# An eight-core transformer layer: one shared SBUF arena split by data type, rotary tables kept in DRAM, three attention panel buffers in place of four

## The reference

```python
x = L0_attn_x                                   # (4, 4096, 2048) float32
x = x + layernorm(attn(layernorm(x)))           # latent attention, 16 heads of 128, causal
x = x + layernorm(ffn(layernorm(x)))            # int8 weights with scales, 8192 wide

def attn(x):
    q = x @ Wq + bq
    kv = x @ Wdown                              # 2048 -> 512
    k, v = kv @ Wk_up, kv @ Wv_up               # 512 -> 2048
    q, k = q*cos + rotate_half(q)*sin, k*cos + rotate_half(k)*sin
    p = softmax(causal(q @ k.T / sqrt(128)))
    return (p @ v) @ Wo + bo

def ffn(x):
    return (silu((x @ w_gate)*s_gate) * ((x @ w_up)*s_up)) @ w_down * s_down
```

## Time and profile before

| | us |
|---|---|
| median of 2 runs | 6633.36 |
| lowest and highest | 6477.97, 6788.75 |
| the profiled execution, whole time | 6477.97 |
| its span on the slowest core (core 3) | 6476.4 |
| spans of the 8 cores | 6450.2 to 6476.4 |
| PE busy in the span | 4436.6 (69%) |
| DVE, ACT, POOL busy | 1560.7, 1398.4, 824.7 |

### The profile page before, as it was taken

How to read it: one execution, slowest core, us unless ns; L and a number is a source line. 1 busy time by engine, 2 the same in 40 slices (tenths; PEclk the granted TensorE clock), 3 DMA queues, 4 the chain that set the end, 5 groups by cost and what they waited for, 6 DMA issues and landing times.

```text
span 6476.4 us, 67826 instructions; the slowest of 8 cores (6450.2 to 6476.4 us)
## 1 busy us (share of the span) xinstructions
PE 4436.6 (69%) x21376; PEld 2020.8 (31%) x21376; DVE 1560.7 (24%) x2965; ACT 1398.4 (22%) x3067; POOL 824.7 (13%) x956
## 2 busy tenths in 40 slices
PE   0144344386666666645546998699986999879985
PEld 0011111132333333422212443244432444334432
DVE  0243334254333333323331110111102110021101
ACT  0212211012666666632221010011001100011000
POOL 0021112142000000000001111111111111111111
PEclk9877677697777777767778999899998999989998
DMA  8423332623777777762229995599947996499944
GB/s 185 114 89 103 96 102 87 142 58 92 146 148 148 151 147 147 151 154 86 83 94 159 151 155 133 137 165 153 149 127 156 156 149 131 127 166 156 150 124 130
DMA packets 1541560, 858.04 MB, mean 132 GB/s; under 512 B 776930, under 2 KB 1516258, under 8 KB 1525474
## 3 DMA queue, kind: packets, MB, share of 16 engines
q0 software_dynamic: 679296, 434.14, 39.7%
q1 hardware_dynamic: 839842, 327.28, 22.5%
q10 hardware_dynamic: 22080, 92.28, 4.2%
HBM read 373.37 MB, written 109.05 MB: 74 GB/s over the span
## 4 chain that ended last, share of the span: by engine, by line
PE 44%; DMA 19%; DVE 11%; ACT 11%; issue 9%; POOL 3%; SPq 2%; ACTq 0%; DVEq 0%; POOLq 0%
PE ps L1043 14%; PE ps L1057 14%; PE ps L1110 8%; DMA arena<-wd 7%; ACT arena L775 7%; DMA ctxr<-xin 3%; PE ps L873 2%; PE ps L446 2%; DMA arena<-arena 2%; PE ps L747 2%; DVE smalls L769 2%; POOL arena L630 2%; PE ps L708 1%; DVE arena L481 1%; DMA arena<-wo 1%
## 5 line engine op out<-in xcount | busy, mean ns | idle before, releaser
L1043 PE MATMUL ps<-arena 128*128 128x512 bf16 x4096 | 934.5, 382 | 198.3 <-DMA arena<-wg 138.0
L1110 PE MATMUL ps<-arena 128*128 128x512 bf16 x4096 | 916.3, 379 | 141.4 <-DMA arena<-wd 140.7
L1057 PE MATMUL ps<-arena 128*128 128x512 bf16 x4096 | 925.8, 379 | 0.0
L775 ACT ACTIVATE arena<-ps,smalls 128x512 bf16<-128x512 f32 (+1 forms) x1152 | 748.4, 667 | 471.3 <-DVE smalls L769 339.0
L747 PE MATMUL ps<-arena 128*128 128x512 bf16 (+1 forms) x1152 | 485.9, 483 | 416.6 <-ACT arena L775 337.1
L1043 PEld LDWEIGHTS ps<-arena 128*128 128x128 bf16 x4096 | 402.6, 98 | 689.1 <-issue 211.8
L1110 PEld LDWEIGHTS ps<-arena 128*128 128x128 bf16 x4096 | 386.3, 97 | 670.8 <-issue 239.4
L412 PE MATMUL ps<-arena 128*128 128x512 bf16 x512 | 129.5, 417 | 663.2 <-DVE arena L421 427.9
L1073 DVE TENSOR_SCALAR ctxr<-ps,smalls 128x512 bf16<-128x512 f32 x256 | 192.1, 750 | 1500.4 <-PE ps L1057 1500.4
L1057 PEld LDWEIGHTS ps<-arena 128*128 128x128 bf16 x4096 | 400.8, 98 | 483.3
L1068 ACT ACTIVATE ctxr<-ps,smalls 128x512 bf16<-128x512 f32 x256 | 175.9, 687 | 1562.5 <-PE ps L1043 1562.5
(11 more groups left out here) (75 smaller groups left out, 2819.5 us busy)
## 6 DMA issues: line engine op xcount, KB each, us to landing
arena<-wg POOLq DMA_DIRECT2D x128, 1024.0 KB, 7.1
arena<-wu POOLq DMA_DIRECT2D x128, 1024.0 KB, 7.2
arena<-wd POOLq DMA_DIRECT2D x256, 512.0 KB, 3.8
ctxr<-xin SPq DMA_DIRECT2D x32, 1024.0 KB, 5.9
xnf_scr<-arena SPq DMA_DIRECT2D x16, 1024.0 KB, 7.1
k_scr<-ctxr SPq DMA_DIRECT2D x16, 1024.0 KB, 7.1
v_scr<-ctxr SPq DMA_DIRECT2D x16, 1024.0 KB, 7.4
arena<-k_scr ACTq DMA_DIRECT2D x16, 1024.0 KB, 5.8
```

The lines of the kernel that those rows point to most:

```text
L775: s.activation(P_b[par][:, n0:n0 + N], psa[:, 0:N], ACT.Exp, bias=negc[:, par:par + 1], scale=1.0, accum_out=lacc[:, par * 8 + ci: par * 8 ...
L1043: rr = t.matmul(ga, wg_s[slp][:, fc, icw * 128:(icw + 1) * 128], x1nfm[:, fc, :], start=(fc == 0), stop=(fc == NH - 1))
L1057: rr = t.matmul(ua, wu_s[slp][:, fc, icw * 128:(icw + 1) * 128], x1nfm[:, fc, :], start=(fc == 0), stop=(fc == NH - 1))
L1110: rr = t.matmul(psa, f_b[:, quar * 4 + ic, j * 128:(j + 1) * 128], wd_s[qp][:, ic, :], start=(quar == 0 and ic == 0), stop=(quar == 15 and ...
```

## The change

One idea runs through it: on-chip memory is now two tensors of one type each, `arF` (12,800 float32 a partition) and `arB` (45,056 bfloat16), beside `ctxr`; no tile is a bit-cast view any more. The tiles are dealt out anew, and since less fits at a time, four things are done otherwise.

- **Tables.** `build_tbl` reads both parts of the K and the Q tables in pieces of 1024 columns (512 KB each) on SP, DVE adds them, SP writes the sum to new DRAM tensors; one pair of buffers `tb1`, `tb2` serves all 12 pieces (4 + 4 + 2 + 2). All of it stands at the start of stage A, before the `wo` conversion's writes and the loads of x on SP. Stages A and B load the slices of 512 columns that a group or round needs (256 KB each, two a group or round, double-buffered) from the ACT queue. Stage B no longer loads or adds tables. The `wo` conversion goes through `xnfm1`, whose first load need not wait for a table.
- **Attention.** Three `P_b` and three `PT_b` in place of four, `par` counts modulo 3, and the context matmuls are emitted when more than two panels are pending, so behind the scores of the panel two after it.
- **Stage D.** The residual sum is written over `tmpd` (no `x1td`), the second layer norm goes to a bfloat16 tile of its own.
- **Stage E.** `sd_b` is replaced by slices of 256 KB, loaded from the ACT queue at the start of each `og` (16 in all, double-buffered); the last normalization is done in place (no `tmpe`); `f_b` lies in `ctxr`, and the float32 tiles `dout` and `x1te` in `arF`.

The core of the diff:

```diff
+    ck_scr = scratch("ck_scr", [128, SEQ], F32)
+    sk_scr = scratch("sk_scr", [128, SEQ], F32)
+    cq_scr = scratch("cq_scr", [128, TOK], F32)
+    sq_scr2 = scratch("sq_scr2", [128, TOK], F32)
...
-    AR_U = 69632
+    ARF_U = 12800
+    ARB_U = 45056
     CTX_U = 32768
-    arena = e(nc.sbuf_tensor("arena", [128, AR_U], BF16))
+    arF = e(nc.sbuf_tensor("arF", [128, ARF_U], F32))
+    arB = e(nc.sbuf_tensor("arB", [128, ARB_U], BF16))
     ctxr = e(nc.sbuf_tensor("ctxr", [128, CTX_U], BF16))
-    smalls = e(nc.sbuf_tensor("smalls", [128, 512], F32))
+    smalls = e(nc.sbuf_tensor("smalls", [128, 256], F32))
...
-        ca = Carver(arena, AR_U)
-        cosk = ca.take([SEQ], F32)
-        sink = ca.take([SEQ], F32)
-        tblt_off = ca.off
-        tblt = ca.take([SEQ], F32)
-        xnfm_off = ca.off
-        xnfm0 = ca.take([NH, 512], BF16)
-        xnfm1 = ar_view(arena, tblt_off, [NH, 512], BF16)
+        cf = Carver(arF, ARF_U)
+        x_t = [cf.take([DM]) for _ in range(3)]
+        rot = [cf.take([512]) for _ in range(2)]
+        m1 = [cf.take([512]) for _ in range(2)]
+        cslc = [cf.take([512]) for _ in range(2)]
+        sslc = [cf.take([512]) for _ in range(2)]
+        tb1 = cf.take([1024])
+        tb2 = cf.take([1024])
+        ca = Carver(arB, ARB_U)
+        wdn_s = ca.take([NH, LAT])
+        wku_s = ca.take([4, DM])
+        wvu_s = ca.take([4, DM])
+        xnfm0 = ca.take([NH, 512])
+        xnfm1 = ca.take([NH, 512])
         xnfm2 = [xnfm0, xnfm1]
-        kvl2 = [ca.take([4, 512], BF16) for _ in range(2)]
-        rot = [ca.take([512], F32) for _ in range(2)]
-        m1 = [ca.take([512], F32) for _ in range(2)]
-        wdn_s = ca.take([NH, LAT], BF16)
-        wku_s = ca.take([4, DM], BF16)
-        wvu_s = ca.take([4, DM], BF16)
+        kvl2 = [ca.take([4, 512]) for _ in range(2)]
         cc = Carver(ctxr, CTX_U)
-        x_t = [cc.take([DM], F32) for _ in range(3)]
-        xn_tm = [cc.take([DM], BF16) for _ in range(2)]
-        kst = cc.take([NH, 512], BF16)
-        vst = cc.take([NH, 512], BF16)
+        xn_tm = [cc.take([DM]) for _ in range(2)]
+        kst = cc.take([NH, 512])
+        vst = cc.take([NH, 512])
         assert cc.off <= CTX_U
...
-        for dst, hi, lo, slot in ((cosk, ckh, ckl, s_cosk),
-                                  (sink, skh, skl, s_sink)):
-            e1 = st("Q", lambda q, d=dst, h=hi: q.dma_start(d, h), dma="dQ")
-            e2 = st("Q", lambda q, l=lo: q.dma_start(tblt, l),
-                    waits=prod_waits(s_tbl), dma="dQ")
-            ev = st("V", lambda v, d=dst: v.tensor_add(d, d, tblt),
-                    waits=[e1, e2])
-            slot.produced(ev)
-            s_tbl.used(ev)
-
-        tblt_b = ar_view(arena, 16384, [NH, 512], BF16)
+        def build_tbl(hi, lo, dst_scr, width):
+            for s0 in range(0, width, 1024):
+                e1 = st("Q", lambda q, hi=hi, s0=s0: q.dma_start(
+                    tb1, hi[:, s0:s0 + 1024]), waits=prod_waits(s_tb1),
+                    dma="dQ")
+                s_tb1.produced(e1)
+                e2 = st("Q", lambda q, lo=lo, s0=s0: q.dma_start(
+                    tb2, lo[:, s0:s0 + 1024]), waits=prod_waits(s_tb2),
+                    dma="dQ")
+                s_tb2.produced(e2)
+                ev = st("V", lambda v: v.tensor_add(tb1, tb1, tb2),
+                        waits=[e1, e2])
+                s_tb1.produced(ev)
+                s_tb2.used(ev)
+                ew = st("Q", lambda q, d=dst_scr, s0=s0: q.dma_start(
+                    d[:, s0:s0 + 1024], tb1), waits=[ev], dma="dQ")
+                s_tb1.used(ew)
+
+        build_tbl(ckh, ckl, ck_scr, SEQ)
+        build_tbl(skh, skl, sk_scr, SEQ)
+        build_tbl(cqh, cql, cq_scr, TOK)
+        build_tbl(sqh, sql, sq_scr2, TOK)
+
         for og in range(4):
             def fnc(g, og=og):
                 sap = bass.AP(wo.tensor, og * 512,
                               [[DM, 128], [128 * DM, NH], [1, 512]])
-                return g.dma_start(tblt_b, sap)
-            ev = st("G", fnc, waits=prod_waits(s_tbl), dma="dG")
-            s_tbl.produced(ev)
+                return g.dma_start(xnfm1, sap)
+            ev = st("G", fnc, waits=prod_waits(s_xnfm2[1]), dma="dG")
+            s_xnfm2[1].produced(ev)
 
             def fnw(q, og=og):
                 dap = bass.AP(wo_scr.tensor, og * 512,
                               [[DM, 128], [128 * DM, NH], [1, 512]])
-                return q.dma_start(dap, tblt_b)
-            ev = st("Q", fnw, waits=cons_waits(s_tbl), dma="dQ")
-            s_tbl.used(ev)
-        s_xnfm2[1].users = list(s_tbl.users)
-        s_xnfm2[1].ready = list(s_tbl.ready)
+                return q.dma_start(dap, xnfm1)
+            ev = st("Q", fnw, waits=cons_waits(s_xnfm2[1]), dma="dQ")
+            s_xnfm2[1].used(ev)
...
+            ev = st("S", lambda s, kg=kg, kgp=kgp: s.dma_start(
+                cslc[kgp], ck_scr[:, kg * 512:(kg + 1) * 512]),
+                waits=prod_waits(s_cslc[kgp]), dma="dA")
+            s_cslc[kgp].produced(ev)
+            ev = st("S", lambda s, kg=kg, kgp=kgp: s.dma_start(
+                sslc[kgp], sk_scr[:, kg * 512:(kg + 1) * 512]),
+                waits=prod_waits(s_sslc[kgp]), dma="dA")
+            s_sslc[kgp].produced(ev)
...
-        for dst, hi, lo, slot in ((cosq, cqh, cql, s_cosq),
-                                  (sinq, sqh, sql, s_sinq)):
-            e1 = st("Q", lambda q, d=dst, h=hi: q.dma_start(d, h), dma="dQ")
-            e2 = st("Q", lambda q, l=lo: q.dma_start(tbltB, l),
-                    waits=prod_waits(s_tbl), dma="dQ")
-            ev = st("V", lambda v, d=dst: v.tensor_add(d, d, tbltB),
-                    waits=[e1, e2])
-            slot.produced(ev)
-            s_tbl.used(ev)
-
         def bload(r):
             rp = r % 2
+            ev = st("S", lambda s, r=r, rp=rp: s.dma_start(
+                cslq[rp], cq_scr[:, r * 512:(r + 1) * 512]),
+                waits=prod_waits(s_cslq[rp]), dma="dA")
+            s_cslq[rp].produced(ev)
+            ev = st("S", lambda s, r=r, rp=rp: s.dma_start(
+                sslq[rp], sq_scr2[:, r * 512:(r + 1) * 512]),
+                waits=prod_waits(s_sslq[rp]), dma="dA")
+            s_sslq[rp].produced(ev)
...
-        ccv = Carver(arena, AR_U)
-        k_s = [ccv.take([SEQ], BF16) for _ in range(2)]
-        v_t = [ccv.take([32, 128], BF16) for _ in range(2)]
-        q_s = [ccv.take([TOK], BF16) for _ in range(2)]
-        P_b = [ccv.take([SEQ], BF16) for _ in range(4)]
-        PT_b = [ccv.take([32, 128], BF16) for _ in range(4)]
-        mks_s = ccv.take([NH, 256], F32)
-        ctx = ar_view(ctxr, 0, [NH, DM], BF16)
+        ccv = Carver(arB, ARB_U)
+        k_s = [ccv.take([SEQ]) for _ in range(2)]
+        v_t = [ccv.take([32, 128]) for _ in range(2)]
+        q_s = [ccv.take([TOK]) for _ in range(2)]
+        P_b = [ccv.take([SEQ]) for _ in range(3)]
+        PT_b = [ccv.take([32, 128]) for _ in range(3)]
+        cfv = Carver(arF, ARF_U)
+        mks_s = cfv.take([NH, 256])
+        ctx = ar_view(ctxr, 0, [NH, DM])
 
         s_k = [Slot(), Slot()]
         s_v = [Slot(), Slot()]
         s_q = [Slot(), Slot()]
-        s_P = [Slot() for _ in range(4)]
-        s_PT = [Slot() for _ in range(4)]
+        s_P = [Slot() for _ in range(3)]
+        s_PT = [Slot() for _ in range(3)]
...
-                par = pancnt % 4
+                par = pancnt % 3
...
-                if len(pend) > 3:
+                if len(pend) > 2:
...
-                x1td, tmpd, xtd[xp]),
+                tmpd, tmpd, xtd[xp]),
...
-            eln3 = ln_soup(x1td, tmpd.bitcast(BF16)[:, 0:DM], s_x1, s_tmp,
-                           [ev_w1])
+            eln3 = ln_soup(tmpd, x1nt, s_x1, s_tmp, [ev_w1])
...
-        ce = Carver(arena, AR_U)
-        wg_s = [ce.take([NH, 256], BF16) for _ in range(2)]
-        wu_s = [ce.take([NH, 256], BF16) for _ in range(2)]
-        f_b = ce.take([64, 512], BF16)
-        wd_s = [ce.take([4, 512], BF16) for _ in range(2)]
-        x1nfm2 = [ce.take([NH, 512], BF16) for _ in range(2)]
+        ce = Carver(arB, ARB_U)
+        wg_s = [ce.take([NH, 256]) for _ in range(2)]
+        wu_s = [ce.take([NH, 256]) for _ in range(2)]
+        wd_s = [ce.take([4, 512]) for _ in range(2)]
+        x1nfm2 = [ce.take([NH, 512]) for _ in range(2)]
+        g_sb = ce.take([512])
+        u_sb = ce.take([512])
         cc = Carver(ctxr, CTX_U)
-        dout = cc.take([4, DM], F32)
-        x1te = cc.take([DM], F32)
-        tmpe = cc.take([DM], F32)
-        sd_b = cc.take([DM], F32)
-        g_sb = cc.take([512], BF16)
-        u_sb = cc.take([512], BF16)
+        f_b = cc.take([64, 512])
+        cfe = Carver(arF, ARF_U)
+        dout = cfe.take([4, DM])
+        x1te = cfe.take([DM])
+        sd_sl = [cfe.take([512]) for _ in range(2)]
...
+                ogp = og % 2
+                ev = st("S", lambda s, og=og, ogp=ogp: s.dma_start(
```

(49 more changed lines are left out.)

63 lines of the change are left out of this document (29 added, 34 removed).

## The result

| | before | after |
|---|---|---|
| median, us (13 and 14 runs) | 6562.79 | 6728.37 |
| lowest, us | 6477.97 | 6666.61 |
| ratio of undisturbed runs, 95% interval | | 1.0276 (1.0236 to 1.0315) |

The kernel became slower by 2.8%. The forecast of 6637 us had the direction and nearly the size (+2.5%), but the measured median, 6728, lies above its range, which ended at 6715. The ratio puts the changed kernel at 6478 x 1.0276 = 6657, its lowest run is 6667, and both lie in the range.

The account below looks back on a forecast made before the run. It saw different limits by stage: serial start-up on SP's queue, DMA at stage B's start, neither ACT nor PE full in stage C. 6478 + 66 - 11 + 99 + 5 = 6637 us, +2.5%, range 6560 to 6715.

Parts of the forecast that it names:

- start-up: Before the first load of x: 12 serial table pieces on SP end at 150 us instead of 84.1, +66, bounds +41 and +92.
- stage C: Attention: late transposes hold up scores, 63 us at heads' ends plus 36 in mid-head, +99, bounds 71 and 124.
- the third buffer suffices: Rival for stage C: delayed panels catch up in ACT's and PE's idle time, C costs nothing, total 6538; chance 0.15.
- The base: The sum starts from the profiled execution, 6477.97 us, not the median of the two runs shown, 6633.36.
- stage E: 16 slices of down scales delay `wd` loads by up to 0.9 us each, 14 in all; +5 taken.
- stage B: Start of stage B: four table loads leave a DMA-busy stretch, two slices enter; -11, bounds 0 and -18.
- The price of a quiet piece (10.2): Start-up: one undisturbed table piece, two loads, sum, write and queue hops, takes 10.2 us.
- the factor of 1.5: Start-up: transfers beside the weights take 1.5 times as long, making a table piece 14.4 us.
- a sign of being wrong: Start-up: a table piece under 9 or over 15 us would show the prediction wrong.
- The Trainium skill's price of a transfer: Start-up: 2.0 us plus bytes at 436 GB/s gives 9.2 us a piece, start-up +29, total 6600.
- the transposes do not get quicker: Stage C: transposes keep their duration; that of a head's widest panel takes 6.7 to 10.3 us.
- several us to spare: Stage C: all panels other than those at heads' ends and before tt = 8 have this cover, so lose nothing.

Follow-up runs that it names:

- experiment 2: The kernel before with four buffers kept, but context matmuls emitted behind the scores of the panel two after instead of three: stage C mean 1343 us against 1252 before.
- experiment 3: The changed kernel with its three buffers, but context matmuls behind the scores of the panel three after: stage C mean 1266 us, lowest whole time 6698.44.
- experiment 7: The changed kernel with POOL's weight loads held until the last table write: quiet pieces 9.5 to 11.0 us by core, tables end at 118 to 134 us.
- experiment 10: The kernel before with three x loads first on SP, table loads on ACT behind the first normalizations, `wo` conversion in eight pieces: ratio 0.9878 (0.9795 to 0.9960).
- experiment 4: The changed kernel with the down scales loaded once at the start of stage E instead of 16 slices: stage E mean 2972 us, whole time 6647.21, ratio 1.023.
- experiment 9: The changed kernel with context matmuls behind the scores of the panel three after and down scales loaded once: lowest run 6571.95, ratio 1.0126.
- Experiment 5: The changed kernel with its 16 slices, but each round's first 1 MB load of `x1te` issued ahead of them: stage E mean 2989 us.
- experiment 6: The changed kernel with table pieces of 2048 columns instead of 1024, through the buffers of x: first load of x at 201 to 212 us against 231 to 246.

## Why the prediction was right and where it failed

- **Direction and main cause, right.** The two large terms, start-up and stage C, were named and make up 163 of the 178 us. The rival that the third buffer suffices is refuted as posed: with the order changed, the loss comes even with four buffers (experiment 2). But with the old order three buffers nearly suffice (experiment 3), so its title was closer to the truth than its chance.
- **The base, the step that put the time outside the range.** "The sum is made against the profiled execution, 6477.97 us" took the lower of two runs that lay 311 us apart. Over 13 runs the median of the kernel before is 6562.79, 85 us above that base, and the range, 6560 to 6715, had no share for it; the median of 14 runs after fell 13 us above its upper end. Set against the measured median of before, the forecast +2.5% comes out as measured (6728.37 / 6562.79 = 1.025). No mechanism of the change is behind this miss.
- **The sum, partly lucky.** 159 against 178 us looks close because errors cancel: stage E was 22 us too low, start-up 11 and stage B 5, while stage C was 13 too high, and the 10 us that came back in stage D and ahead of stage E had been put at nothing.
- **Start-up, +66 forecast, +77 measured.** The price of a quiet piece (10.2) was right: 9.5 to 11.0 by core (experiment 7). The step that was mis-sized is the factor of 1.5 for transfers beside the weights, taken from a single transfer of 2 MB. For a string of small ones it was larger: the first two intervals are 29.5 and 25.1 us against 14.4 forecast, beyond the 15 us that the prediction itself had named as a sign of being wrong. That it did not cost more is because fewer pieces fell in the crowded stretch, about 4 instead of 5.8, and it thinned out sooner.
- **The Trainium skill's price of a transfer** (DMA: Bandwidth & Descriptors, Anatomy of one DMA) is fitted to transfers that GpSimd issues; for a piece, which SP issues, it gave 9.2 us as an estimate. The quiet pieces of experiment 7 take 9.5 to 11.0, so the measurement decides against it, on core 6 by little.
- **Stage B, -11 and -6.** Between the bounds. The DMA engines stay 96% busy there after the change, in 77 us instead of 84. One reason given for 11 instead of 18 does not hold: 1 MB of x in 5.85 us is 179 GB/s, less than the 210 of that stretch and not more. No run takes the table loads out of stage B alone, so the cause is argued.
- **Stage C, +99 and +86.** Both places and the order of waits were right, PE's waits at 50 places too. At the head's end 3.5 us were lost and 4.2 forecast. Over 120 changes of head the 32 matmuls take 3.28 us in the mean instead of 2.29, and the longer wait adds one panel, 3.1 us: both as forecast. What was wrong is "the transposes do not get quicker": that of the widest panel lands after 7.0 us in the mean instead of 7.4 (7.1 in experiment 2), for a reason that was not followed up, and the narrower panel behind the wait is done 0.1 us sooner. In mid-head 2.2 us were lost and 2.4 forecast, but not all before tt = 8: 0.5 of it is the transpose of tt = 4, which the forecast had left with "several us to spare". It lands after about 7 us in either kernel, where those of tt = 3 and 5 take 3 to 4; SP issues the transposed load of V right behind it.
- **Stage D, 0 and -5.** Not explained. Experiment 10, whose stage D is that of the kernel before, has 513 to 521 us too, against 519 to 523 in the trace before, so it need not be the change's doing at all.
- **Ahead of stage E, 0 and -5.** The forecast counted the 16 slices and not the 1 MB load that they replace. Experiments 4 and 9 bring the load back and the 5 us with it.
- **Stage E, +5 and +27: the term of the sum that failed.** The upper bound, 14 us, was also too low. I priced the slices by their bytes (0.9 us each) and let a third of them collide. Even the price was off: at the rate named, 1 MB of x in 5.85 us, 256 KB are 1.5 us, and 16 of them 23. Experiment 5 puts the slices alone at about 17 us. Two of the four of a round go out at group 0's start; the other two go out at the starts of groups 1 and 2, in the same microsecond in which a `wd` load is issued, and there the first step takes 5.7 us. That makes about 2 us for each of these eight. And the text said nothing of `x1te`: adding waits to ACT's queue moved everything behind them, and the 1 MB load, which had gone out at group 0's start, went out with the slice of group 3. What is queued behind a new wait was asked of SP and POOL and not of ACT in stage E.

## What to carry to other kernels

In an engine with a written order, the distance between producing and consuming is part of the program: here a lead of three panels instead of two is worth 75 us with three buffers and 91 with four, and moving the consumer ahead of the step that reuses its buffer bought it without memory. When a transfer with a wait is added to a queue, list the transfers behind it and ask when they go out now; when one is taken away, ask what it stood in front of. And a serial string of small loads, sums and writes at the start of a program costs its full length, more than its length while bulk loads run beside it; put what the first compute step needs first.

## What the runs showed of the hardware that was not expected

- Beside POOL's converting weight loads (the DMA engines 93% busy in the first 84 us of core 7), a table piece that takes 9.2 to 12.0 us alone took up to 29.5; twice the bytes took up to 34.8 (experiments 6 and 7). The delay goes with the transfer more than with its bytes.
- In the same crowd a transposing DMA of 128x2048 landed 36.4 us after its issue (experiment 10, core 2; 35 to 40 on all cores). Later in stage A such a transpose lands after 4.3 in the median, 10.4 at most on that core.
- When a 256 KB and a 1 MB load went out within 1 us of a 512 KB `wd` load, they landed after 5.2 and 8.9 us and the `wd` load after 7.0, where the one before had taken 3.9.
- Behind waits of PE of 4.2 and 4.3 us the granted clock was 0.50 for the next matmuls, behind one of 1.2 us it was 1.00, so a late transfer cost PE its wait and a microsecond or more of slow matmuls on top.
